# Loading the weights first in a step of a cross-attention and mixed-expert kernel, and turning them by column groups

## The reference

```python
def layer(x, ctx):                       # x: 16 x 112 x 256, ctx: 16 x 375 x 256, float32
    x = x + xattn(layernorm(x), ctx)     # 16 heads of 16, softmax over 375 keys
    x = x + ffn(layernorm(x))
    return x

def ffn(h, gW1, gb1, gW2, gb2, eW1, eb1, eW2, eb2):    # H = 256, DFF = 1024, E = 8
    x = transpose(h, (1, 0, 2))          # 112 "batches" of 16 tokens
    g = (relu(x @ gW1.T + gb1) @ gW2.T + gb2).mean(axis=1)     # 112 x 8
    W1 = einsum('be,eoi->boi', g, eW1);  b1 = g @ eb1          # a weight matrix for each of 112
    W2 = einsum('be,eoi->boi', g, eW2);  b2 = g @ eb2
    y = relu(x @ W1.T + b1) @ W2.T + b2
    return transpose(y, (1, 0, 2))
```

## Time and profile before

| | |
|---|---|
| median of 3 runs | 946.9 us (937.15 to 949.12) |
| profiled execution | 942.49 us, of which span 940.7 us |
| TensorE busy | 755.9 us (80%) |
| VectorE, ScalarE, GpSimd busy | 546.2 us, 499.9 us, 373.2 us |
| mean granted clock of TensorE | 0.909 |
| moved by DMA | 146.26 MB, packets under 512 B: 84954 of 128016 |

### The profile page before, as it was taken

The page is one execution under the profiler, slowest core; times in us unless marked ns, Lnnn a source line. Parts: engine busy times, 40 slices in busy tenths (PEclk is TensorE's granted clock), DMA queues, the critical chain, the costliest instruction groups (busy, mean ns, idle before and its releaser), DMA issues.

```text
span 940.7 us, 38323 instructions
## 1 busy us (share of the span) xinstructions
PE 755.9 (80%) x16407; PEld 612.4 (65%) x16407; DVE 546.2 (58%) x796; ACT 499.9 (53%) x779; POOL 373.2 (40%) x483
## 2 busy tenths in 40 slices
PE   3788999999977877588888887887887888888792
PEld 2656777778756645466676676766665676676672
DVE  6766776777756455355556645654555466466581
ACT  3645767676744546355556545554545455555450
POOL 7543545455564652224324323423422342342200
PEclk9989999999989787699999989998899799899897
DMA  6468666666655608765456566565455646655523
GB/s 191 108 174 205 178 175 160 175 166 170 164 127 126 162 7 170 168 180 161 142 166 194 153 165 181 154 175 171 126 154 154 188 139 172 192 142 152 184 71 80
DMA packets 128016, 146.26 MB, mean 155 GB/s; under 512 B 84954, under 2 KB 105546, under 8 KB 121602
## 3 DMA queue, kind: packets, MB, share of 16 engines
q1 hardware_dynamic: 127874, 144.14, 56.6%
HBM read 102.78 MB, written 41.03 MB: 153 GB/s over the span
## 4 chain that ended last, share of the span: by engine, by line
PE 43%; DMA 22%; SPq 21%; DVE 5%; issue 4%; POOL 3%; ACT 1%; ACTq 0%; POOLq 0%; DVEq 0%
PE banks L1735 12%; SPq L668 12%; DMA w_nat<-in_w 12%; PE banks L1701 9%; DMA k_stack<-k_dram 8%; PE banks L1556 5%; PE banks L316 4%; SPq L651 4%; PE banks L1438 3%; PE banks L1397 3%; PE banks L1420 2%; PE banks L1755 2%; SPq L511 2%; SPq L518 1%; PE banks L1487 1%
## 5 line engine op out<-in xcount | busy, mean ns | idle before, releaser
L1290 DVE COPY wb<-banks 128x896 f32<-128x896 f32 x231 | 251.6, 1089 | 239.7 <-PE banks L1701 239.5
L1080 ACT ACTIVATE wb<-banks 128x896 f32<-128x896 f32 x281 | 254.4, 917 | 170.5 <-PE banks L1701 170.3
L831 POOL CAST w_split<-w_rest 128x1024 bf16<-128x1024 f32 x32 | 33.2, 1036 | 340.8 <-ACT w_rest L960 278.7
L1701 PE MATMUL banks<-spread,ring 64*128 64x112 bf16 x4096 | 159.4, 222 | 8.5 <-DMA ring<-split_dram 3.6
L1701 PEld LDWEIGHTS banks<-spread,ring 64*128 64x128 bf16 x4096 | 114.9, 100 | 64.7 <-issue 56.2
L1162 DVE TENSOR_REDUCE maxima<-banks 112x2 f32<-112x750 f32 x128 | 118.0, 935 | 32.7 <-PE banks L1397 30.0
L1556 PE MATMUL banks<-ident,w_nat 128*128 128x128 f32 x256 | 53.0, 371 | 98.2 <-DMA w_nat<-in_w 97.9
L1735 PE MATMUL banks<-wb,ht 128*32 128x128 f32 x3584 | 127.3, 284 | 2.1 <-issue 2.1
L1735 PE MATMUL banks<-wb,xt 128*32 128x128 f32 x3584 | 126.8, 284 | 0.3 <-issue 0.2
L886 ACT ACTIVATE probs<-banks 128x448 f32<-128x448 f32 x192 | 100.7, 544 | 29.8 <-PE banks L1420 27.9
L1556 PEld LDWEIGHTS banks<-ident,w_nat 128*128 128x128 f32 x256 | 42.5, 209 | 102.4 <-issue 100.1
(11 more groups left out here) (133 smaller groups left out, 970.2 us busy)
## 6 DMA issues: line engine op xcount, KB each, us to landing
ring<-split_dram SPq DMA_DIRECT2D x384, 128.0 KB, 3.3
split_dram<-w_split SPq DMA_DIRECT2D x32, 768.0 KB, 5.3
k_dram<-k_parts SPq DMA_DIRECT2D x16, 576.0 KB, 3.6
k_stack<-k_dram SPq DMA_DIRECT2D x32, 288.0 KB
w_nat<-in_w SPq DMA_DIRECT2D x32, 256.0 KB, 4.1
w_nat<-in_w SPq DMA_DIRECT2D x64, 128.0 KB, 3.1
k_stack<-k_dram SPq DMA_DIRECT2D x32, 192.0 KB
c_raw<-in_ctx_t SPq DMA_DIRECT2D x16, 375.0 KB, 5.2
```

The source lines that it names most:

```text
L1080: act.activation(outputs_of(n, q), formed(bank), ACT.Copy).then_inc(form_act, 1)
L1290: dve.tensor_copy(outputs_of(n, q), formed(bank))\
L1701: last = pe.matmul(banks[:, form_bank(half) + t, NQ * r:NQ * r + NQ], ring[rows, 4 * q + r, :], spread[rows], start=True, stop=True)
```

## The change

It has four parts.

- **Natural loads.** `w_nat` is one tile of 8 experts x 128 columns instead of two halves of 64 columns, so that a run in memory and in the tile is 512 bytes long instead of 256, and an "in" chunk takes one DMA (before: two), an "out" chunk two (before: four). In the loop the load comes first in SP's step, ahead of ring half 0. In the front the loads of chunks 1 to 3 go out early in steps 14 to 16 instead of at the end.
- **The turn.** Eight transposes of 128 columns per chunk become 32 plain matmuls of 32 columns, four for each result, on the four column groups. The weights are read 64 bytes apart (before: 32), and the forms' results are written to `wb` at other columns (`outputs_of`), in pieces of four elements as before.
- **GpSimd's order.** The cut of the biases goes ahead of `inverse_root` in step 12. Splits 0 and 1 move from the ends of steps 13 and 14 to the places ahead of `inverse_root` in steps 14 and 15, split 2 from behind the memset of `xt` to the end of step 16, and the memset of `ring` from step 14 to the end of step 13. `store_split(2)` goes ahead of the ring loads of chunk 1.
- **y.** Its eight loads leave the place ahead of the loop: four are issued in period 0, four in period 1, behind the store.

```diff
@@ -162,7 +162,7 @@
 
         lasting = Region(start, at_keep)
         ring = lasting.take("ring", [P, P // 2, P], BF16)
-        w_nat = lasting.take("w_nat", [P, 2, E, P // 2], F32)
+        w_nat = lasting.take("w_nat", [P, E, P], F32)
         w_split = lasting.take("w_split", [P, 3, 8, P], BF16)
         w_rest = lasting.take("w_rest", [P, 8, P], F32)
         spread = lasting.take("spread", [P, NQ], BF16)
@@ -469,7 +469,7 @@
 
         def outputs_of(n, q):
 
-            return wb[n % 2][:].rearrange("p b (k t) -> p b k t", k=2)[:, :, :, 4 * q:4 * q + 4]
+            return wb[n % 2][:].rearrange("p b (k t x r) -> p b k t x r", t=2, x=2, r=4)[:, :, q // 2, :, q % 2, :]
 
         block = stack.enter_context(nc.Block())
 
@@ -589,6 +589,8 @@
                 if b.exists_from(2):
                     load_queries(b, 1)
                     load_keys(b, 1)
+                if s.i is None and TURN_STEP < s.c <= TURN_STEP + 3:
+                    load_natural(s.c - TURN_STEP)
                 if s.exists_from(1):
                     load_maxima(s, 1)
                 load_context(s + 4)
@@ -623,33 +625,25 @@
                     for n, piece in enumerate(PRODUCT_PARTS):
                         sp.dma_start(eb_ring[n:TILE:SLOTS], eb_parts[:, piece]).then_inc(eb_ready, 16)
                 if s.i is None and s.c == TURN_STEP + 1:
-                    load_natural(1)
                     store_split(0)
                 if s.i is None and s.c == TURN_STEP + 2:
-                    load_natural(2)
                     load_ring(0, 0)
                     load_ring(0, 1)
                     store_split(1)
-                if s.i is None and s.c == TURN_STEP + 3:
-                    load_natural(3)
 
             def load_natural(m):
                 if not turns_alive(m):
                     return
                 need(sp, turn_mm, 2 * m)
                 kind, i, a = ORDER[m]
-                for t in range(2):
-                    cols = slice(P // 2 * t, P // 2 * t + P // 2)
-                    if kind == "in":
-                        src = w1.rearrange("(e s) p k n -> p e s k n", s=2)[:, :, i // 4, a,
-                                                                           P * (i % 4):P * (i % 4) + P]
-                        sp.dma_start(w_nat[:, t], src[:, :, cols]).then_inc(nat_loaded, 16)
-                        continue
-                    src = w2.rearrange("(e c) p k n -> p e c k n", c=OT // 2)[:, :, i // 2, i % 2, :]
-                    for part in range(2):
-                        half = src.rearrange("p e (j n) -> p e j n", j=2)[:, :, part, P * a:P * a + P]
-                        sp.dma_start(w_nat[:, t].rearrange("p (e j) n -> p e j n", j=2)[:, :, part],
-                                     half[:, :, cols]).then_inc(nat_loaded, 16)
+                if kind == "in":
+                    src = w1.rearrange("(e s) p k n -> p e s k n", s=2)[:, :, i // 4, a, P * (i % 4):P * (i % 4) + P]
+                    sp.dma_start(w_nat[:], src).then_inc(nat_loaded, 16)
+                    return
+                src = w2.rearrange("(e c) p k n -> p e c k n", c=OT // 2)[:, :, i // 2, i % 2, :]
+                for part in range(2):
+                    half = src.rearrange("p e (j n) -> p e j n", j=2)[:, :, part, P * a:P * a + P]
+                    sp.dma_start(w_nat[:].rearrange("p (e j) n -> p e j n", j=2)[:, :, part], half).then_inc(nat_loaded, 16)
 
             def store_split(m):
                 if turns_alive(m):
@@ -670,23 +664,27 @@
 
             steps(sp, step)
 
+            store_split(2)
             load_ring(1, 0)
             load_ring(1, 1)
-            store_split(2)
             for slot in range(2):
                 sp.wait_ge(xmid_stored[slot], 16 * B // 2)
             sp.wait_ge(xt_mm, B)
             mids = xmid_dram.rearrange("(s h j g) c -> h j s g c", h=2, j=4, g=GRP)
-            for j in range(4):
+
+            def load_y(j):
                 for h in range(2):
                     at = 32 * j + B * h
                     sp.dma_start(y[at:at + B], mids[h, j]).then_inc(y_loaded, 16)
 
             outs = out.rearrange("(s h j g) c -> h j s g c", h=2, j=4, g=GRP)
             for n in range(CHUNKS):
+                load_natural(n + TURN_AHEAD + 1)
                 load_ring(n + 2, 0)
-                load_natural(n + TURN_AHEAD + 1)
                 store_split(n + TURN_AHEAD)
+                if n < 2:
+                    load_y(2 * n)
+                    load_y(2 * n + 1)
                 load_ring(n + 2, 1)
                 if n == CHUNKS - 1:
                     unit_taken(sp, value_unit(n - 1, UNITS - 1))
@@ -800,29 +798,33 @@
                 b = s + 3
                 if b.exists_from(EARLY + 1):
                     context_low(b)
+                if s.i is None and s.c == TURN_STEP - 1:
+                    split_biases()
+                if s.i is None and s.c in (TURN_STEP + 1, TURN_STEP + 2):
+                    split(s.c - TURN_STEP - 1)
                 b = s + -1
                 if b.exists:
                     need(pool, bits_halved, b.times(1, 1) + ROOTS)
                     inverse_root(0, 1, b.times(ROOT_OPS) + ROOT_OPS * ROOTS)
-                if s.i is None and s.c == TURN_STEP - 1:
-                    for g in range(NG):
-                        queries_stored(pool, g)
-                    pool.wait_ge(stack_set, 16)
-                    pool.memset(eb_ring[:], 0.0).then_inc(eb_zeroed, 1)
-                    pool.wait_ge(eb_loaded, 16)
-                    pool.tensor_copy(eb_parts[:, 0], eb_rest[:]).then_inc(eb_cut, 1)
-                    pool.wait_ge(eb_cut, 1)
-                    pool.tensor_tensor(eb_rest[:], eb_rest[:], eb_parts[:, 0], ALU.subtract).then_inc(eb_cut, 1)
-                    pool.wait_ge(eb_cut, 2)
-                    pool.tensor_copy(eb_parts[:, 1], eb_rest[:]).then_inc(eb_cut, 1)
-                    pool.wait_ge(eb_cut, 3)
-                    pool.tensor_tensor(eb_parts[:, 2], eb_rest[:], eb_parts[:, 1], ALU.subtract).then_inc(eb_cut, 1)
                 if s.i is None and s.c == TURN_STEP:
-                    split(0)
-                if s.i is None and s.c == TURN_STEP + 1:
                     pool.wait_ge(eb_ready, 16 * PRODUCTS)
                     pool.memset(ring[:].rearrange("p s i -> p (s i)").bitcast(F32), 0.0).then_inc(ring_zeroed, 1)
-                    split(1)
+                if s.i is None and s.c == TURN_STEP + 3:
+                    split(2)
+
+            def split_biases():
+                for g in range(NG):
+                    queries_stored(pool, g)
+                pool.wait_ge(stack_set, 16)
+                pool.memset(eb_ring[:], 0.0).then_inc(eb_zeroed, 1)
+                pool.wait_ge(eb_loaded, 16)
+                pool.tensor_copy(eb_parts[:, 0], eb_rest[:]).then_inc(eb_cut, 1)
+                pool.wait_ge(eb_cut, 1)
+                pool.tensor_tensor(eb_rest[:], eb_rest[:], eb_parts[:, 0], ALU.subtract).then_inc(eb_cut, 1)
+                pool.wait_ge(eb_cut, 2)
+                pool.tensor_copy(eb_parts[:, 1], eb_rest[:]).then_inc(eb_cut, 1)
+                pool.wait_ge(eb_cut, 3)
+                pool.tensor_tensor(eb_parts[:, 2], eb_rest[:], eb_parts[:, 1], ALU.subtract).then_inc(eb_cut, 1)
 
             def split(m):
                 if turns_alive(m):
@@ -840,7 +842,6 @@
 
             pool.wait_ge(xt_done, B)
             pool.memset(xt[:, :, :, 1, :], 0.0).then_inc(pads_set, 1)
-            split(2)
             pool.wait_ge(spread_done, 1)
             for h in range(2):
                 gates = spread[:, PAIRS * h:PAIRS * h + PAIRS].rearrange("e (j g) -> e g j", j=4)
@@ -1549,12 +1550,14 @@
                 else:
                     unit_taken(pe, turn_unit(m, w) - 2)
                 if w == 0:
-                    pe.wait_ge(nat_loaded, 16 * (2 * (m + 1) + 2 * OUTS_UPTO[m + 1]))
+                    pe.wait_ge(nat_loaded, 16 * (m + 1 + OUTS_UPTO[m + 1]))
                 bank = turn_bank(m, w)
                 for k in range(4):
                     q = 4 * w + k
-                    last = pe.transpose(banks[:, bank, P * k:P * k + P],
-                                        w_nat[:].rearrange("p t e (o q) -> p (t e o) q", q=8)[:, :, q], ident[:])
+                    for c in range(4):
+                        left = w_nat[:].rearrange("p e (k t q) -> p t q (e k)", t=2, q=8)[:, c // 2, q]
+                        last = pe.matmul(banks[32 * c:32 * c + 32, bank, P * k:P * k + P],
+                                         left[:, 32 * (c % 2):32 * (c % 2) + 32], ident[:], start=True, stop=True)
                 last.then_inc(turn_mm, 1)
 
             def last_steps(s):
```

## The result

The changed kernel takes 885.4 us (median of 4 runs, 881.2 to 889.7), the kernel before, in the same session, 944.6 us (4 runs, 937.2 to 949.1): ratio 0.938, 95% interval 0.929 to 0.947. It is faster, by 59 us; I had forecast 844 us and a range from 824 to 878. The profiled execution took 889.2 us with a span of 887.3, where the forecast for that execution was 839.8: 49.4 us are missing.

The account below looks back on a forecast made before the run. TensorE was taken as the bound in work, stopped by one late `w_nat` load in nearly every period; -77.8, -11.8 and -13.1 us, together -102.7, took 942.49 to 839.8, in proportion 844 us, range 824 to 878.

Parts of the forecast that it names:

- The sum: Whole kernel: -77.8 us in periods 5 to 27, -11.8 in 1 to 4, -13.1 in period 0; together -102.7.
- What is late next: Loop: after `w_nat`, `ring` comes close (0.45 us of waits per period), then `w_split`, 12 us against a period of 13.4.
- the clock term: Periods 5 to 27: granted clock 0.91 loses 37.2 us of TensorE's 339.9 busy, leaving 302.7 us of warm work.
- the price of the turn: Periods 5 to 27: the new turn adds 0.95 us in each of 23 periods.
- The ring waits: Periods 5 to 27: TensorE waits 0.45 us per period for `ring`, 10.4 us in all.
- The price of the wait: TensorE's 97.9 us wait for `w_nat` before the turns costs its own time and the slower clock behind it.
- Load first: SP's loop step: issued first, the natural load lands by 10 us, before the turn at 13.4; the 97.9 us wait goes.
- The turn by column groups: TensorE's turn: 64 records at 32 ns take 2.05 us against 1.16 warm, adding 0.9 us per turn.
- y in two steps: First periods: period 0's 14.85 us wait goes; `y` loads may cost 1 to 2 us in periods 1 to 4.
- The front: Stretch ahead of the loop: gains and losses, including a stall ending 1.6 us later, sum to 0, between -5 and +5.
- The ring becomes the bound: Rival in the loop: `ring` lands too late in some 20 periods, +18 to +32 us, say 868; 0.25 with the store loop.
- The rival on unoverlapped weight reads: Turn: 64-byte steps make 64 records take 114 ns each, 7.3 us instead of 2.05; +168, some 1010 us; chance 0.02.

Follow-up runs that it names:

- e2: The kernel before with one line moved: the natural load issued first in SP's loop step, ahead of ring half 0; 862.4 us, ratio 0.917.
- e6: The changed kernel with only the turn undone (old layout of `w_nat`, its loads of 256-byte runs, 8 transposes); 859.5 us, ratio 0.919 to the kernel before.
- e4: The changed kernel with the turn made of 16 matmuls of 64 columns instead of 32 of 32; 864.2 us, ratio 0.922 to the kernel before.
- e3: The changed kernel with all eight `y` loads issued ahead of the loop, before `store_split(2)` and the second ring; 877.1 us, ratio 0.934 to the kernel before.
- e1: The changed kernel with the loop's natural load issued behind ring half 0 again, as before; 977.7 us, ratio 1.043 to the kernel before.

## Why the prediction was wrong

**The step that failed is "The sum", in its term for periods 5 to 27, and the list under "What is late next".** I asked which data comes too late when `w_nat` no longer does, named `ring` and `w_split`, and gave the supply of TensorE's own instructions nothing. It costs 43.1 us in these periods. Taken with the other terms of that row: 371.7 - 43.1 - 2.4 (all other steps over 0.2 us) = 326.2 us of warm work, where I had 302.7 + 23 x 0.95 = 324.6. So the clock term, the price of the turn and the wait taken away were right together, to 2 us. The ring waits were 10.4 in the sum and 0.4 in the trace of these periods, a miss of 10 to the other side.

- *The price of the wait*: right. e2 alone took it away and gave 0.917.
- *Load first*: right; `w_nat` holds nobody, and a period without a stall, 496.81 to 510.16, takes 13.35 us (13.4 forecast).
- *The turn by column groups*: its own time right (1.98 us; 2.05 forecast), its price wrong. Beside 0.9 us a turn it fills the last stretch of the period that used few instructions: e6 and e4 show 23 and 29 us at the marks that hang on it. I had counted its records (16 instructions become 128) only to multiply them by 32 ns.
- *y in two steps*: wrong. I gave it 1 to 2 us and it costs about 10: 6.48 up to 380.81 and 3.32 up to 398.48, and beyond these the clock behind both (0.79 and 0.62 in the two windows above). The stall of 14.85 in period 0 is gone, as said.
- *The front*: -1.7, inside -5 to +5, with the bias cut about 5 us instead of 1.6 and other parts better.
- *The rivals*: none of them was this one. "The ring becomes the bound" came nearest (868, against 885.4 measured) by a mechanism that did not occur, and the measured time lies above the whole range. The rival on unoverlapped weight reads is refuted: 33 ns per record at 64 bytes between elements.

The evidence was in the profile of before. The queue of instruction packets stands on its page, and the trace has stops of 1.08 us at 784.48 and of 0.67 at 534.47, inside a group of forms and both at marks, in a kernel that stopped for 3 us in nearly every period:

```profile
q8 instruction: 116, 1.90, 0.9%
...
534.47 0.22 PE L1701 MATMUL banks<-spread,ring 64*128 64x112 bf16 x1 [0.67 <-issue]
...
784.48 0.22 PE L1701 MATMUL banks<-spread,ring 64*128 64x112 bf16 x2 [1.08 <-issue]
```

At the marks of that kernel the next instructions had landed 2.5 us before (median), against 1.4 to 1.5 us in the changed one. I read such "issue" rows as noise because they were small, and didn't ask what they would be without the pause.

## What to carry to other kernels

Before a wait is taken away, look what else used the pause: here it was TensorE's instruction supply, one 16 KB packet for 256 matmuls and weight loads, which a stream of small matmuls at 16 ns an instruction uses up in 4 us. An idle that the profile calls "issue" in the middle of a group, and a multiple of 256 records from the next one, is such a stop; fewer and wider matmuls lessened it (43 to 14 us) though they were no faster by themselves. And a change in several parts is to be tried part by part: one moved line gave more than all of it.

## What the runs showed of the hardware

- Instruction packets: 83 for 21158 matmul and weight-load records, 16 KB each; in periods 5 to 27 of the changed kernel all 26 steps that are over 0.7 us late with no semaphore wait stand where one begins, up to 2.1 us each. Behind four `y` loads of 224 KB that go to 16 partitions each it was 6.5 us, behind eight of them 5.1 (e3).
- From the end of such a packet to the first matmul that waited for it: 1.2 to 1.8 us at 378 stops of fourteen traces. The packets took 0.9 to 1.9 us to move in the changed kernel.
- A float32 weight load of 64 columns takes 196 ns and of 32 columns 138 (e4, e3), and the turn takes the same time with either. With elements 64 bytes apart the load of 32 columns lasts 138 ns where those of `wb` last 109 and 111, which costs nothing in the turn's time at 33 ns per record.
- A matmul stream behind a pause pays twice. The turn of 64 records takes 1.98 us at a clock of 1.00 (at 496.81) and 3.45 at 0.54 behind a wait of 3.89 us (e1):

```profile
483.45 3.45 PE L1559 MATMUL banks<-ident,w_nat 128*32 128x128 f32 x64 [3.89 <-DMA w_nat<-in_w]
```
